# Last attention of a four-layer network: the value products of two steps done together in every other step

## The reference

```python
h = _group_norm(x, gn_scale, gn_bias)
h = jnp.einsum('bchw,cd->bdhw', h, W_qkv) + b_qkv[None, :, None, None]
h = h.reshape(B, num_heads, 3 * hd, H * W).transpose(0, 1, 3, 2)
q, k, v = jnp.split(h, 3, axis=-1)
logits = jnp.einsum('bhsd,bhtd->bhst', q, k) * scale
attn = jax.nn.softmax(logits, axis=-1)
vals = jnp.einsum('bhst,bhtd->bhsd', attn, v)
h = vals.transpose(0, 1, 3, 2).reshape(B, C, H, W)
h = jnp.einsum('bchw,cd->bdhw', h, W_out) + b_out[None, :, None, None]
return x + h
```

## Time and profile before

| | |
|---|---|
| median of 3 runs | 4758.0 us (4751.83 to 4764.63) |
| profiled execution, own time | 4763.85 us |
| profiled execution, span | 4762.0 us |
| mean granted TensorE clock | 0.947 |
| TensorE matmul busy | 4295.8 us (90%) |
| DVE, ACT, POOL busy | 2984.6, 2638.3, 1866.5 us |

### The profile page before, as it was taken

The page is one execution under the profiler, slowest core; times in us unless marked ns, Lnnn a source line. Parts: engine busy times, 40 slices in busy tenths (PEclk is TensorE's granted clock), DMA queues, the critical chain, the costliest instruction groups (busy, mean ns, idle before and its releaser), DMA issues. The chain is left out here.

```text
span 4762.0 us, 71270 instructions
## 1 busy us (share of the span) xinstructions
PE 4295.8 (90%) x19523; PEld 2386.1 (50%) x19523; DVE 2984.6 (63%) x4089; ACT 2638.3 (55%) x4655; POOL 1866.5 (39%) x1579
## 2 busy tenths in 40 slices
PE   2699999999999999999998999469998977969888
PEld 1355555555555555555557777224444433434443
DVE  7777777777777777777775333637666633244442
ACT  3588888888888888888884333211111110112221
POOL 1545444444444444444442555212222200025553
PEclk7799999999999999999999999789999977979999
DMA  1200000000000000000001000098666611442211
GB/s 41 117 2 2 2 2 2 2 2 2 2 2 2 2 2 2 2 2 2 2 2 36 0 0 0 21 337 307 217 229 221 211 42 64 148 99 61 63 36 71
DMA packets 97302, 280.44 MB, mean 59 GB/s; under 512 B 33120, under 2 KB 34144, under 8 KB 78016
## 3 DMA queue, kind: packets, MB, share of 16 engines
q0 software_dynamic: 20736, 151.00, 8.9%
q1 hardware_dynamic: 76480, 128.39, 8.8%
HBM read 224.37 MB, written 54.85 MB: 59 GB/s over the span
## 5 line engine op out<-in xcount | busy, mean ns | idle before, releaser
L495 POOL TENSOR_TENSOR cpb_sum<-cpb_parts 128x512 f32<-128x512 f32 x768 | 799.2, 1048 | 795.3 <-DVE cpb_r L659 770.1
L654 ACT ACTIVATE cpb_h<-cpb_z,net_vec 128x512 f32<-128x512 f32 x1536 | 1061.8, 691 | 49.6 <-PE cpb_z L613 0.4
L610 PE MATMUL cpb_z<-cpb_r,cpb_w2a 128*128 128x512 f32 x2048 | 1043.1, 509 | 0.2 <-ACTq L636 0.2
L659 DVE SCALAR_TENSOR_TENSOR cpb_r<-cpb_z,cpb_r 128x512 fp32r<-128x512 f32 x1283 | 884.5, 690 | 246.8 <-ACT cpb_r L624 223.3
L624 ACT ACTIVATE cpb_r<-cpb_z 128x512 fp32r<-128x512 f32 x1283 | 756.7, 602 | 200.8 <-PE cpb_z L551 200.8
L611 PE MATMUL cpb_z<-cpb_r,cpb_w2b 128*128 128x512 f32 x2048 | 805.7, 393 | 0.0
L613 PE MATMUL cpb_z<-cpb_r,cpb_w2a 128*128 128x512 f32 x2048 | 803.4, 392 | 0.0
L659 DVE SCALAR_TENSOR_TENSOR cpb_r<-cpb_sum,cpb_r 128x512 fp32r<-128x512 f32 x768 | 578.3, 753 | 273.2 <-ACT cpb_r L624 273.2
L1413 PE MATMUL dc_pc<-dc_sc,l_dcw 128*128 128x512 f32 x1152 | 530.8, 605 | 6.5 <-ACT dc_dc L1468 6.5
L551 PE MATMUL cpb_z<-cpb_exp,l0k_w1p 128*128 128x512 bf16 x1283 | 498.6, 389 | 0.0
L624 ACT ACTIVATE cpb_r<-cpb_sum 128x512 fp32r<-128x512 f32 x768 | 481.6, 627 | 0.0
(11 more groups left out here) (323 smaller groups left out, 5247.3 us busy)
## 6 DMA issues: line engine op xcount, KB each, us to landing
corners<-cf_tt SPq DMA_DIRECT2D x77, 256.0 KB, 3.5
qk_parts<-gn_r SPq DMA_DIRECT2D x64, 256.0 KB, 2.0
l_dcw<-in_dc_wT SPq DMA_DIRECT2D x9, 1024.0 KB, 10.8
bias_dram<-cpb_bst SPq DMA_DIRECT2D x520, 8.0 KB
net_x<-in_x SPq DMA_DIRECT2D x8, 1024.0 KB, 8.7
sa_qa<-qk_parts SPq DMA_DIRECT2D x16, 512.0 KB, 9.0
sa_ka<-qk_parts SPq DMA_DIRECT2D x16, 512.0 KB, 10.9
l_w<-in_mlp_w1T SPq DMA_DIRECT2D x1, 4096.0 KB, 23.4
```

The source lines that it names most:

```text
L495: pool.tensor_tensor(SUM[:, n % 4, :].rearrange("p (y x) -> p y x", x=W), PARTS[:, slot, key, 0:1, :].broadcast_to([P, H // 2, W]), PARTS[ ...
L610: pe.matmul(z2[:, bank, :], W2A[:], R1[:, k, :], start=True, stop=False)
L654: act.activation(H2[:, t % 8, :], z2[:, t % 3, :], ACT.Relu, bias=V("cpb_b2")).then_inc(h2a, 1)
L659: return v.scalar_tensor_tensor(R2[:, t % 4, :], first_layer(t), 0.0, R1[:, t % 4, :].bitcast(F32), ALU.max, ALU.subtract)
```

## The change

At even steps from 2 on, the values of the two steps before are done, at odd steps none; step 0 of a pair does those of steps 14 and 15 of the pair before, and after the last pair both are done. Nothing else is changed, on no other engine either.

```diff
-                    if c:
+                    if c % 2 == 0 and c:
+                        values(pair, c - 2)
                         values(pair, c - 1)
-                    elif pair:
+                    elif c == 0 and pair:
+                        values(pair - 1, STEPS - 2)
                         values(pair - 1, STEPS - 1)
                     if c == 3 and pair:
                         sums(pair - 1, 1)
                     if c == 11:
                         sums(pair, 0)
+            values(GS - 1, STEPS - 2)
             values(GS - 1, STEPS - 1)
             sums(GS - 1, 1)
```

## The result

| | before | changed |
|---|---|---|
| median | 4759.59 us (12 runs, 4751.83 to 4764.85) | 4770.65 us (12 runs, 4762.98 to 4776.71) |
| ratio | | 1.0023, 95% interval 1.0014 to 1.0032 |
| profiled execution, span | 4762.0 us | 4773.5 us |
| second passes, first sp to last sums | 471.1 us | 483.0 us |
| period of a plain pair | 58.77 us (no half-clock stretch in it) | 61.21 us (one, behind the transpose of step 14) |

The forecast was 4761, the range 4749 to 4775. The time lies in the range and 10 us above the point; the direction was right, the size was not: 11 us instead of 2.5. (Lines behind the edit have shifted by 3: L2089 is L2086 of before, L2098 is L2095.)

The account below looks back on a forecast made before the run. TensorE's program order was taken to set the pace. +0.5 us for six middle pairs, +0.4 for pair 0, +1.6 for the last and 0 for the clock gave +2.5 on 4758.0, rounded 4761; range 4749 to 4775.

Parts of the forecast that it names:

- The order of the units and the values: Middle pairs on TensorE, segment by segment: new waits and savings nearly cancel, +0.1 us a pair, +0.5 for six.
- c0 to c3: Step 0 to the start of step 3 in a middle pair: 11.72 becomes 13.02 us, +1.30.
- to fp6: Sums to first-pass unit 6: DVE's chain of 6.37 us still sets the pace, change 0.
- to c7: First-pass unit 6 to step 7: 7.74 becomes 8.13 us, +0.39.
- The price of the switch: Two values blocks together save one entry and exit of the 64-column shape, 0.28 us; second block 0.91 after the first.
- rival D: Values after values still cost 1.01 us and the entry is paid too: 3 us more, 4764; chance 0.08.
- fp15 to c0': Chain from first-pass unit 15 to the next pair's step 0: 8.32 us before, shorter by 0.59, to 7.73.
- ACT's copy 3.3 after fp15: Sign in the timeline: ACT's copy starts 3.3 us after first-pass unit 15 instead of 3.90.
- The clock: Half-clock stretches of the second-pass stage, 14 before, 21 us in all: change taken as 0, bounds -10 and +15.
- rival B: New 0.53 us waits near steps 2 and 6 bring half-clock stretches, 10 more, 15 us: 4776; chance 0.10.
- Rival C: Saved mode-switch drains count in full, 64 x 0.28 = 18 us faster, 4740; chance 0.05.
- The last pair: No first pass there, so even steps' second passes wait for exp, delaying POOL's second half and the end: +1.6 us.

Follow-up runs that it names:

- run 1: Changed kernel, POOL's first add of step 14 made to wait until DVE has split the maxima; 4773.0 us.
- run 2: Changed kernel, values of step 12 back at step 13, step 14 doing only those of step 13; 4783.5 us.
- run 7: run 1 with useless matmuls in TensorE's waits, five between the units of steps 2 and 6, four before step 0; 4741.9 us.
- run 3: Kernel before, POOL's adds of step 13 held until the last first-pass unit has left TensorE; 4756.5 us.
- run 9: Changed kernel with useless matmuls, five between the units of steps 2 and 6, eight before the transpose of step 14; 4765.8 us.
- run 6: Kernel before, five useless matmuls in the wait between the two units of steps 2 and 6; 4750.2 us.
- run 4: Kernel before, only values of step 2 moved to step 4 and of step 10 to step 12; 4745.1 us.
- run 5: run 4 with the values of steps 2 and 6 placed between their two units; 4733.0 us.
- run 10: run 5 with four useless matmuls in the wait for the maxima before step 0; 4723.4 us.

## Why the prediction was right or wrong

**The order of the units and the values: right.** The segments of a pair in the changed kernel (4353.68 to 4414.89), measured against forecast: c0 to c3 12.90 (13.02), to the sums 2.07 (2.06), to fp6 6.51 (6.37), to c7 8.05 (8.13), to c11 12.94 (13.04), to the sums 2.05 (2.06), to fp15 6.51 (6.37). Each is within 0.14 us. The price of the switch was right too: the second block of values starts 0.91 us after the first, and two blocks before a second pass take 1.87 us, where I had 1.92. That rules out rival D.

```profile
4387.82 1.94 PE L2013 MATMUL sa_po<-net_x,sa_vs 128*64 128x512 f32 x8
4389.69 0.50 PE L2004 MATMUL sa_pb<-sa_qa,sa_ka 128*128 128x512 f32 x1
```

**fp15 to c0': wrong, and this is the step that failed.** I wrote that the transpose is bound by DVE at 2.96 us, with 0.21 and 0.23 for the two small operations, and that the copy follows at 3.31. The sum holds where POOL is idle, which is where I had read it (pair 0). But the same sentence moved exp of step 14 forward by 1.09 us, and POOL's adds follow exp. I counted who waits for that exp on ACT and not who starts because of it. The copy came at 5.26 (4404.71 to 4409.97), 1.95 us later than forecast. Of the signs that I had given, "ACT's copy 3.3 after fp15" is the one that failed. Runs 1, 2 and 7 take the cause away and both operations are short; run 3 puts it into the kernel before and one of them is long; run 9 removes most half-clock stretches and they stay long. With POOL out of the way the chain is 7.69 us (run 1), where the forecast had 7.73.

The Trainium skill has it in SBUF — State Buffer, section Who interferes with whom: a DVE instruction with two SBUF inputs, or a cast in a two-port mode, can't run beside a GpSimd instruction that reads SBUF, and whoever comes first keeps the port to its end. This case agrees: each of the 35 slow operations of the changed kernel and of runs 3 and 9 ends 0.03 to 0.04 us after an add. In which mode the cast ran, no run here shows. That page speaks against the change, and I did not weigh it. With what it costs here the sum would have been 0.1 + 1.95 = 2.05 us a pair; the measured period without a stretch is 60.79 against 58.77, 2.02 more.

**The clock: taken as 0, which came out near, by luck of place.** The clock's part grew from 26.1 to 31.4 us, but part of it lies where TensorE waits anyway. If each pair is set against the same pair without a stretch (runs 3, 6 and 9 have them), the stretches cost 22.0 us in the kernel before and 18.4 in the changed one. The changed kernel has a stretch behind the transpose in each of the seven pairs, in the chain of the maxima: there the two blocks of values take up to 3.5 instead of 1.9 us, but step 0 would have waited for the DMA, and the chain grows by 0.4 only (10.18 against 9.75 in run 9). With POOL out of the way, the same order has a clock's part of 43 us (run 1), and of 2.4 with filled waits (run 7). So a loss of the kind of rival B was there once the other one was taken away. That its new waits did it is not shown: in run 1 step 0 lost 1.6 us as well (5.5 instead of 3.9), behind a wait that is old. Nor does any run show why the same wait is followed by a stretch in one pair and not in the next.

**Rival C, the drains saved**, is bounded by run 7: with POOL out of the way the new order gains at most 0.2 us a pair at full clock, of which 0.15 are the fillers. The saving is real (0.91 from one block of values to the next) and is paid back in waits for the maxima.

**The last pair.** Forecast +1.6; it took 40.2 us from step 0 to the last sums against 40.4 before, but the one before holds a half-clock stretch. In run 3, which has TensorE's old order and no stretch there, it takes 38.9. The change costs 1.3 us in it.

**The size.** Without half-clock stretches the change costs the stage 15.6 us: 2.02 in each of pairs 1 to 6 (58.77 to 60.79), 2.2 in pair 0 (57.53 in run 6, 59.73 in run 9), 1.3 in the last. The forecast of 2.5 and seven times the 1.95 that it lacked are 16.2. The stretches gave 3.6 back, and 12.0 are left; the stage grew by 11.9, the medians by 11. This account is of single executions, and how much the stretches give or take in another is open. The time lies in the stated range, but not for the reason that the range was made for: its upper part was held for half-clock stretches, and no rival had POOL in it. That is luck.

## What to carry to other kernels

When work on one engine is moved, follow the engines that get their work earlier by it, not only those that get it later: here POOL's adds started 1 us sooner and fell on two small operations of DVE in the longest chain. Look for a wait before you look for a cheaper order: moving values into waits that existed (runs 4 and 5) gave 26 us, about 19 of them at full clock (58.77 to 56.07 a pair), while the order that saved mode switches gave nothing at full clock even with POOL out of the way. And price a wait of TensorE by what the clock does after it as well; where it can't be removed, matmuls that do nothing were worth 5 to 31 us here (runs 6, 7, 9 and 10).

## What was not expected of the hardware

- An operation of 128x16 elements on DVE took 1.17 to 1.21 us instead of 0.17 or 0.18, ending 0.03 to 0.04 us after POOL's add of 128x512 beside it; the max reductions out of PSUM, which ran beside adds all the time, stayed at 1.22 us.
- Useless matmuls in waits made a kernel faster: 4759 to 4750 (run 6), 4773 to 4742 (run 7), 4733 to 4723 (run 10), with the granted clock of the stage up from 0.94 to 0.97 and from 0.91 to 0.99 in the first two.
- How often the half clock comes can outweigh the order: run 1, whose stage is 7.7 us shorter apart from the clock's part, was no faster than the changed kernel, with periods of 64.6 to 65.0 us in five pairs running, against 58.6 in run 7.
